# Edge pass of a graph attention kernel: the masked sum moves from the end of TensorE's step to its front

## The chip, the cores and the metric

The kernel runs on one core of a Trainium2 chip. Times are device microseconds (us) of one launch. A core has five engines that run their own instruction streams and meet at semaphores: TensorE (PE in the rows, with PEld for its weight loads), VectorE (DVE), ScalarE (ACT), GpSimd (POOL) and SyncE (SP, which here issues DMAs).

## The reference

The input is x with 50,000 rows of 768 numbers and a list of 25,000 edges (src, dst), sorted by dst. First comes a graph attention layer with 12 heads of 64, then a feed-forward layer:

```
def gnn(h, src, dst):                      # h = layernorm(x)
    ft = einsum('nhd,od->nho', h, W)
    e = leaky_relu(a1[src] + a2[dst])      # a1, a2: sums of ft times attention vectors
    w = exp(e - segment_max(e, dst)[dst])
    alpha = w / segment_sum(w, dst)[dst]
    agg = segment_sum(alpha * ft[src], dst)
    return relu(agg + einsum('nhd,od->nho', h, W_res))
x = x + gnn(layernorm(x), src, dst)
x = x + ffn(layernorm(x))                  # 768 -> 96 -> 768 for all but six rows
```

## The kernel before

The program has two long passes and a short passage between them. The **edge pass** computes `alpha * ft[src]` and its sum over edges of one destination, and writes one row of 768 per edge to a scratch tensor in memory, of which the **node pass** gathers what it needs. The node pass (392 tiles of 128 nodes) does the residual product and the feed-forward layer, and the change doesn't touch it.

The edge pass takes the edges in 196 chunks of 128 (`EC`). It is a pipeline written out by hand: every engine runs the same loop over steps c (14 steps in a loop body, `BODY`), and in step c it does the part with lag L for chunk c - L. What is done in which step is set by the `L_` constants, and in which order within a step by the order of the code. Nothing reorders it later. The engines' steps carry the same number c but aren't in lockstep; semaphores tie them.

TensorE's step c, lines 771 to 844: 12 transposes of the gathered source and destination rows of chunk c - 9 (L785), six products with the weights for chunk c - 10 (L794, called ft below), in some steps two small transposes (L811/L812 or L817/L818), six products that give the destination score of chunk c - 10 (L823, called a2 below), and last the masked sum of chunk c - 21 (L835 and L837, `L_SUM` = 21). The masked sum multiplies a 128x128 mask (edges with the same destination) by the weighted messages, and writes 768 columns to `sum_ps`, of which there is one (a second one, `sum2_ps`, is used only for the last ten chunks). So it waits for three things: the messages (`s_msg`), the mask (`s_mask`), and that the sum of the chunk before has been read out (`s_eo`).

VectorE's step c, in this order: small operations of a group of seven chunks (L1015 to L1046), the readout of the sum of chunk c - 22 into `agg_ring` (L1059, called evict below, 128x768; it waits for `s_sum` and for the DMA that wrote out the ring's slot two chunks ago), the messages of chunk c - 20 (L1071), four bn_stats and two bn_aggr of chunk c (L1106 to L1114), then a wait for a2 of the same step (`s_sc`), and behind it the mask of chunk c - 20 (L1128), the score column `e_col` of chunk c - 10 (L1149), and, each in one step of seven, the leaky maximum (L1157), the scans of the maximum (L1132 to L1172), the scans of the sum (L1177 to L1183) and the reciprocal with alpha (L1137 to L1144). The wait stands in the code as

```
                    if exists(cf, EC):
                        dve.wait_ge(s_sc, cf + 1)
```

with cf = c - 10, ahead of the mask. ScalarE reads the transposes (L665) and ft (L671) out of PSUM and normalizes (L651). GpSimd issues three indirect DMAs per chunk: a gather of source rows (L538), one of destination rows (L542) and a scatter of row numbers (L553), 13 to 15 chunks ahead and held back by `s_tr`, `s_sc` and `s_sum`. SyncE writes each evicted chunk to memory (L458).

Of the kernel before, what the change touches and what calls it, by code (L numbers as in the profile page):

```python
# [8 lines left out]
D = 768  # L9
# [5 lines left out]
P = 128  # L15
NC = D // P
# [11 lines left out]
BODY = 2 * G  # L28
EC = -(-N_EDGES // (P * BODY)) * BODY
# [19 lines left out]
L_FT = 10  # L49
L_DT = 20  # L50
L_MSG = 20
L_SUM = 21
# [21 lines left out]
def turns(eng, n, drain):  # L74


    yield 0
    yield 1
    if n > 2:
        with eng.Fori(2, n) as b:  # L80
            yield b
    for b in range(drain):
        yield n + b
# [7 lines left out]
def exists(t, n):  # L91

    return not isinstance(t, int) or 0 <= t < n


def at_least(eng, sem, value):

    if not isinstance(value, int) or value > 0:
        eng.wait_ge(sem, value)


def gnn_ffn_kernel(nc, x, x_cols, edges, dst_rows, dst_next, dst_prev, dst_ends, chunk_base, sel_heads,
# [9 lines left out]
    with ExitStack() as ctx:  # L112
# [3 lines left out]
        def sem(name):  # L116
            return ctx.enter_context(nc.semaphore(name))
# [10 lines left out]
        def part(lo, *shape, rows=P):  # L128
            size = 1
            for s in shape:  # L130
                size *= s
            flat = arena[0:rows, lo:lo + size]
            if len(shape) == 2:
                return flat.rearrange("p (a b) -> p a b", b=shape[1])
            if len(shape) == 3:
                return flat.rearrange("p (a b c) -> p a b c", b=shape[1], c=shape[2])
            return flat
# [4 lines left out]
        ft_ring = part(21504, BODY, NC, FTW)  # L142
        mask_ring = part(32424, 2, P)
# [120 lines left out]
        def sums(b, co):  # L264

            return sum2_ps if isinstance(b, int) and co > EC - L_SUM + L_FT and (EC - 1 - co) % 2 == 1 else sum_ps

        def twice(b, co):

            return 1 if isinstance(b, int) and co > EC - L_SUM + L_FT + 1 else 0  # L270
# [60 lines left out]
        s_eft = sem("s_eft")  # L331
        s_sc = sem("s_sc")
        s_ecol = sem("s_ecol")
        s_mask = sem("s_mask")
# [15 lines left out]
        s_msg = sem("s_msg")  # L350
        s_sum = sem("s_sum")
        s_eo = sem("s_eo")
# [399 lines left out]
        def _(pe):  # L752
# [5 lines left out]
            for c in range(NC):  # L758
                last = nc.tensor.matmul(ps[:, 1, 0:2 * HEADS], ones[:], v_sb[:, OFF * c:OFF * c + OFF],
                                        start=(c == 0), stop=(c == NC - 1))  # L760
# [10 lines left out]
            for b in turns(pe, NB, 2):  # L771
                for i in range(BODY):
                    c = BODY * b + i
                    ct = c - L_TR
                    if exists(ct, EC):
                        v = (i - L_TR) % BODY
                        for k in range(NBLK):
                            if k == 0:
                                pe.wait_ge(s_norm, ct + 1)
                            if k == 1:  # L780
                                pe.wait_ge(d_ge[v], 32 * (b + (i - L_TR) // BODY + 1))
                            at_least(pe, s_etr, NBLK * (ct - 1) + k + 1)
                            for m in range(4 * k, 4 * k + 4):
                                src = xs_ring if m < NC else xd_ring
                                last = nc.tensor.transpose(ps[:, k, m % 4 * P:(m % 4 + 1) * P],  # L785
                                                           src[:, v, m % NC * P:(m % NC + 1) * P], ident[:])
                            last.then_inc(s_tr, 1)
                    cf = c - L_FT
                    if exists(cf, EC):
                        v = (i - L_FT) % 2  # L790
                        pe.wait_ge(s_etr, NBLK * cf + 2)
                        at_least(pe, s_eft, cf)
                        for n in range(NC):
                            last = nc.tensor.matmul(ft_ps[:, n // 3, n % 3, :], both_t[:, v, n * P:(n + 1) * P],  # L794
                                                    wgv[:, n, :], start=True, stop=True)
                        last.then_inc(s_ft, 1)

                    gs_ = 2 * b + (i - 18) // G
                    ga = 2 * b + (i - 20) // G
                    if exists(cf, EC + 1):  # L800
                        at_least(pe, s_ecol, cf)
                    if (i - 18) % G == 0 and exists(gs_, NG):
                        pe.wait_ge(s_same, gs_ + 1)
                    if (i - 20) % G == 0 and exists(ga, NG):
                        pe.wait_ge(s_alpha, ga + 1)
                    gt_ = 2 * b + (i - 17) // G
                    if (i - 17) % G == 0 and exists(gt_, NG):
                        w = (i - 17) // G % 2
                        pe.wait_ge(s_leak, gt_ + 1)
                        pe.wait_ge(s_dsl, gt_ + 1)  # L810
                        nc.tensor.transpose(row_ps[:, 0:P], e_col[:, w, :], ident[:])  # L811
                        nc.tensor.transpose(row_ps[:, P:2 * P], same_x[:, w, :], ident[:]).then_inc(s_ert, 1)  # L812
                    gw_ = 2 * b + (i - 19) // G
                    if (i - 19) % G == 0 and exists(gw_, NG):
                        pe.wait_ge(s_exp, gw_ + 1)
                        pe.wait_ge(s_tot, gw_ + 1)
                        nc.tensor.transpose(w_ps, w_row[:], ident[0:HG, 0:HG])  # L817
                        nc.tensor.transpose(den_ps, m_row[:], ident[0:HG, 0:HG]).then_inc(s_wst, 1)  # L818
                    if exists(cf, EC):
                        v = (i - L_FT) % 2  # L820
                        pe.wait_ge(s_etr, NBLK * cf + NBLK)
                        for n in range(NC):
                            last = nc.tensor.matmul(a2_ps, both_t[:, v, D + n * P:D + (n + 1) * P],  # L823
                                                    v2c[:, n, :], start=(n == 0), stop=(n == NC - 1))
                        last.then_inc(s_sc, 1)
                    co_ = c - L_SUM
                    if exists(co_, EC):
                        v = (i - L_SUM) % BODY
                        pe.wait_ge(s_msg, co_ + 1)
                        pe.wait_ge(s_mask, co_ + 1)  # L830
                        at_least(pe, s_eo, co_ - twice(b, co_))
                        if isinstance(b, int) and co_ == EC - L_SUM + L_FT + 1:
                            pe.wait_ge(s_eft, EC)
                        to = sums(b, co_)
                        nc.tensor.matmul(to[:, 0:4 * P].rearrange("p (a f) -> p a f", f=P), mask_ring[:, v % 2, :],  # L835
                                         ft_ring[:, v, 0:4, 0:P], start=True, stop=True)
                        nc.tensor.matmul(to[:, 4 * P:D].rearrange("p (a f) -> p a f", f=P), mask_ring[:, v % 2, :],  # L837
                                         ft_ring[:, v, 4:NC, 0:P], start=True, stop=True).then_inc(s_sum, 1)
                    if isinstance(b, int) and c == EC + 14:
                        pe.wait_ge(s_eqf, 1)  # L840
                        for n in range(2):
                            last = nc.tensor.matmul(cnt_ps[:, n:n + 1], eq_f[:, n * EH:(n + 1) * EH], ones[:, 0:1],
                                                    start=True, stop=True)
                        last.then_inc(s_cnt, 1)
# [27 lines left out]
            for b in turns(pe, NT // U, 1):  # L872
                for u in range(U):
# [7 lines left out]
                    if exists(tu, NT):  # L881
                        q = b * (U // PAIR) + (u - L_UP) // PAIR
                        v, k = (u - L_UP) // PAIR % 2, (u - L_UP) % PAIR
# [3 lines left out]
                        for i in range(k * NC // PAIR, (k + 1) * NC // PAIR):  # L887
                            for n, (w, h) in enumerate(((w1_hi, t2_hi[:, v]), (w1_lo, t2_hi[:, v]), (w1_hi, t2_lo[:, v]))):
                                last = nc.tensor.matmul(ps[0:HID, 6 + v, 0:PAIR * P], w[:, i, :], h[:, i, :],  # L889
                                                        start=(i == 0 and n == 0), stop=(i == NC - 1 and n == 2))  # L890
# [3 lines left out]
                    if exists(td, NT):  # L894
                        v = (u - L_DOWN) // PAIR % 2
                        f = slice((u - L_DOWN) % PAIR * P, ((u - L_DOWN) % PAIR + 1) * P)
                        pe.wait_ge(s_hlo, b * (U // PAIR) + (u - L_DOWN) // PAIR + 1)
                        at_least(pe, s_o, td)
                        for lo, hi in ((0, 512), (512, D)):
                            for n, (h, w) in enumerate(((h_hi, w2_hi), (h_hi, w2_lo), (h_lo, w2_hi))):  # L900
                                last = nc.tensor.matmul(pair(2)[:, lo:hi], h[:, v, f], w[:, lo:hi],  # L901
                                                        start=(n == 0), stop=(n == 2))
# [14 lines left out]
            for a in range(NEXP):  # L917
                for i in range(NC):
                    last = nc.tensor.matmul(ps[0:HID, 0, a * NCLS:(a + 1) * NCLS], a1_sb[:, i, a, :], cls_t[:, i, :],  # L919
                                            start=(i == 0), stop=(i == NC - 1))  # L920
            last.then_inc(s_ch, 1)
            for i in range(NC):
                last = nc.tensor.matmul(ps[0:NCLS, 1, 0:2 * NCLS], cls_t[:, i, :], gw_sb[:, i, :],
                                        start=(i == 0), stop=(i == NC - 1))
# [3 lines left out]
            for s in range(2):  # L928
                for lo, hi in ((0, 512), (512, D)):
                    for a in range(NEXP):  # L930
                        last = nc.tensor.matmul(pair(1 + s)[0:NCLS, lo:hi], hm[:, s, a, :], a2_sb[:, a, lo:hi],  # L931
                                                start=(a == 0), stop=(a == NEXP - 1))
# [441 lines left out]
```

## Time and profile before

| | before |
|---|---|
| median of 3 runs | 2899.18 us |
| lowest and highest | 2893.96, 2901.88 us |
| the profiled execution's own time | 2880.44 us |
| its span | 2878.2 us |
| edge pass with all parts running, from the end of the last a2 ahead of the first sum to the end of the last a2 | 117.88 to 1133.73 us |
| busy over the span: TensorE, VectorE, ScalarE, GpSimd | 95%, 90%, 76%, 74% |
| mean granted clock of TensorE | 0.978 of full |

The profile is of one execution. Its table gives the busy time of each engine; the timeline gives every instruction with its start, its length and, in brackets, how long its engine had been idle and what ended that. A granted clock of 1.00 in a stretch stands for 2.4 GHz and 0.50 for 1.2 GHz; the values between are means over a stretch in which both occurred.

### The profile page before, as it was taken

The numbers are of one execution on the slowest core, as the hardware profiler recorded it, in microseconds if no ns is written. First come the engines' busy times: TensorE is split into PE (matmuls) and PEld (weight loads), VectorE is DVE, ScalarE is ACT, GpSimd is POOL, SyncE is SP. The second block draws the span as 40 slices with busy tenths as digits, with TensorE's granted clock in tenths as the row PEclk, the third lists the DMA queues.
The fourth block names the chain that finished last, engine by engine and source line by source line (L and its number), as shares of the span: only waits on it lengthen the run. The fifth ranks groups of instructions, "written<-read, shape, count | busy, mean of one in ns | idle before, by whom it ended". The sixth has DMA issues, their size and how long they took to land. (4 is left out here: it accounts for less than half of the span.)

```text
span 2878.2 us, 67583 instructions
## 1 busy us (share of the span) xinstructions
PE 2739.4 (95%) x21062; PEld 2543.4 (88%) x21062; DVE 2579.1 (90%) x5419; ACT 2179.7 (76%) x4157; POOL 2136.6 (74%) x2029
## 2 busy tenths in 40 slices
PE   4789999999999998489999999999999999999998
PEld 4777888888888887389999999999999999999996
DVE  5677899999999996589999999999999999999995
ACT  3545566666666664389999999999999999999982
POOL 6755666677767650388888888888888888888881
PEclk9899999999999999699999999999999999999998
DMA  8999999999888872689999999999999998989973
GB/s 209 173 194 193 219 234 230 235 231 236 233 232 238 231 199 102 232 300 345 341 334 328 328 322 323 319 319 319 318 309 317 314 315 310 312 311 312 309 268 120
DMA packets 254693, 770.85 MB, mean 268 GB/s; under 512 B 79795, under 2 KB 85683, under 8 KB 254355
## 3 DMA queue, kind: packets, MB, share of 16 engines
q1 hardware_dynamic: 181964, 557.25, 55.2%
q0 software_dynamic: 69312, 209.33, 31.9%
q8 instruction: 122, 2.00, 0.3%
q10 hardware_dynamic: 3176, 1.29, 0.2%
q14 instruction: 119, 0.97, 0.1%
HBM read 635.88 MB, written 232.17 MB: 302 GB/s over the span
## 5 line engine op out<-in xcount | busy, mean ns | idle before, releaser
L910 PE MATMUL ps<-wr_bd,arena 128*128 128x128 f32 x4704 | 594.4, 276 | 25.7 <-DVE arena L1254 23.0
L910 PEld LDWEIGHTS ps<-wr_bd,arena 128*128 128x128 f32 x4704 | 564.0, 193 | 28.4 <-issue 25.1
L632 POOL DMA_INDIRECT arena<-agg_scratch,nrow x392 | 440.1, 1123 | 82.2 <-issue 67.7
L665 ACT ACTIVATE arena<-ps 128x512 f32<-128x512 f32 x588 | 308.1, 594 | 189.4 <-PE ps L785 188.8
L610 POOL TENSOR_SCALAR arena<-csr_neg,mv,r_n 128x768 f32<-128x768 f32 x392 | 388.1, 990 | 50.8 <-PE ps L768 36.7
L1249 DVE SCALAR_TENSOR_TENSOR ps<-ps,r_n,arena 128x768 f32<-128x768 f32 x392 | 398.9, 1018 | 19.3 <-PE ps L910 11.2
L1254 DVE SCALAR_TENSOR_TENSOR arena<-ps,arena 128x768 f32<-128x768 f32 x392 | 375.3, 957 | 13.4
L622 POOL TENSOR_SCALAR arena<-arena,nm_n,r_n 128x768 f32<-128x768 f32 x392 | 384.1, 980 | 0.8 <-POOL r_n L601 0.6
L713 ACT ACTIVATE t_hi<-ps 128x768 fp32r<-128x768 f32 x392 | 315.2, 804 | 88.5 <-PE ps L768 88.2
L1261 DVE TENSOR_TENSOR t_lo<-ps,t_hi 128x768 fp32r<-128x768 f32 x392 | 373.7, 953 | 6.7 <-ACT t_hi L713 6.5
L701 ACT ACTIVATE arena<-arena,mv 128x768 f32<-128x768 f32 x392 | 368.0, 939 | 12.7
L1238 DVE TENSOR_TENSOR arena<-arena,ps 128x768 f32<-128x768 f32 x392 | 369.8, 943 | 6.2 <-PE ps L901 6.1
L722 ACT ACTIVATE arena<-arena,s_st 128x768 f32<-128x768 f32 x392 | 364.3, 929 | 11.5 <-DVE arena L1254 11.5
L889 PE MATMUL ps<-t_hi,w_hi 128*96 128x256 f32 x1176 | 360.9, 307 | 0.0
L889 PE MATMUL ps<-t_lo,w_hi 128*96 128x256 f32 x1176 | 330.3, 281 | 0.0
L785 PE MATMUL ps<-ident,arena 128*128 128x128 f32 x2352 | 298.1, 278 | 33.2 <-ACT arena L651 23.2
L889 PE MATMUL ps<-t_hi,w_lo 128*96 128x256 f32 x1176 | 328.7, 280 | 0.0
L768 PE MATMUL ps<-ident,arena 128*128 128x128 f32 x2352 | 322.1, 273 | 5.9 <-POOL arena L622 5.4
L739 ACT ACTIVATE arena<-arena 128x768 f32<-128x768 f32 x392 | 326.1, 832 | 0.6
L785 PEld LDWEIGHTS ps<-ident,arena 128*128 128x128 f32 x2352 | 277.9, 144 | 53.4 <-issue 24.7
L542 POOL DMA_INDIRECT arena<-in_x,e_slot x196 | 192.2, 981 | 173.3 <-PE ps L823 127.5
L794 PE MATMUL ps<-wgv,arena 128*128 128x130 f32 x2352 | 298.5, 276 | 0.0
(199 smaller groups left out, 6361.7 us busy)
## 6 DMA issues: line engine op xcount, KB each, us to landing
arena<-in_x SPq DMA_DIRECT2D x196, 768.0 KB
arena<-in_x_cols SPq DMA_DIRECT2D x392, 384.0 KB, 4.9
out<-arena SPq DMA_DIRECT2D x195, 768.0 KB, 5.7
agg_scratch<-arena SPq DMA_DIRECT2D x196, 384.0 KB, 2.3
dst_all<-in_dst_rows SPq DMA_DIRECT2D x28, 256.0 KB
arena<-in_x,e_slot POOLq DMA_INDIRECT x392, 6.7
arena<-agg_scratch,nrow POOLq DMA_INDIRECT x392
dst_all<-in_dst_rows SPq DMA_DIRECT2D x28, 192.0 KB
```

The costliest lines, as they stand in the source:

```text
L610: pool.tensor_scalar(g_ring[:, g, :].rearrange("p (c f) -> p c f", f=P), csr_neg[:, None, :].to_broadcast([P, NC, P]), mv1[:, w, 2 * (v % ...
L622: pool.tensor_scalar(n2[:, v % 2, :], y_ring[:, v, :], nm_n[:, w, k:k + 1], r_n[:, w, PAIR + k:PAIR + k + 1], ALU.add, ALU.mult).then_inc( ...
L632: pool.indirect_dma_start(g_ring[:, g, :], None, agg_d, bass.IndirectOffsetOnAxis(nrow[:, v:v + 1], 0), bounds_check=EP - 1, oob_is_err=Fa ...
L701: nc.scalar.activation(junk[:, 0, :], x_ring[:, v, :], ACT.Square, bias=mv1[:, w, 2 * k:2 * k + 1], scale=-1.0, accum_out=q_st[:, w, k:k + ...
L722: nc.scalar.activation(junk[:, 1, :], y_ring[:, v, :], ACT.Square, bias=s_st[:, w, k:k + 1], scale=-float(D), accum_out=q_st[:, w, 2 + k:3 ...
L785: last = nc.tensor.transpose(ps[:, k, m % 4 * P:(m % 4 + 1) * P], src[:, v, m % NC * P:(m % NC + 1) * P], ident[:])
L889: last = nc.tensor.matmul(ps[0:HID, 6 + v, 0:PAIR * P], w[:, i, :], h[:, i, :], start=(i == 0 and n == 0), stop=(i == NC - 1 and n == 2))
L910: last = nc.tensor.matmul(pair(1)[:, i * P:(i + 1) * P], xt_ring[:, g, i * P:(i + 1) * P], wr_bd[:], start=True, stop=True)
L1238: V.tensor_tensor(y_ring[:, v, :], y_ring[:, v, :], pair(2), ALU.add).then_inc(s_o, 1)
L1249: V.scalar_tensor_tensor(pair(1), pair(1), r_n[:, w, k:k + 1], g_ring[:, g, :], ALU.mult, ALU.add).then_inc(s_z1, 1)
L1254: V.scalar_tensor_tensor(y_ring[:, v, :], pair(1), 0.0, x_ring[:, v, :], ALU.max, ALU.add, accum_out=s_st[:, w5, k:k + 1]).then_inc(s_y, 1)
L1261: V.tensor_tensor(t2_lo[:, v, :, f], pair(0).rearrange("p (c n) -> p c n", c=NC), t2_hi[:, v, :, f].bitcast(f32), ALU.subtract).then_inc(s ...
```

## The change

The block that makes the masked sum is moved, word for word, from the end of TensorE's step to its front, ahead of the transposes. The lag stays 21.

```diff
             for b in turns(pe, NB, 2):
                 for i in range(BODY):
                     c = BODY * b + i
+                    co_ = c - L_SUM
+                    if exists(co_, EC):
+                        v = (i - L_SUM) % BODY
+                        pe.wait_ge(s_msg, co_ + 1)
+                        pe.wait_ge(s_mask, co_ + 1)
+                        at_least(pe, s_eo, co_ - twice(b, co_))
+                        if isinstance(b, int) and co_ == EC - L_SUM + L_FT + 1:
+                            pe.wait_ge(s_eft, EC)
+                        to = sums(b, co_)
+                        nc.tensor.matmul(to[:, 0:4 * P].rearrange("p (a f) -> p a f", f=P), mask_ring[:, v % 2, :],
+                                         ft_ring[:, v, 0:4, 0:P], start=True, stop=True)
+                        nc.tensor.matmul(to[:, 4 * P:D].rearrange("p (a f) -> p a f", f=P), mask_ring[:, v % 2, :],
+                                         ft_ring[:, v, 4:NC, 0:P], start=True, stop=True).then_inc(s_sum, 1)
                     ct = c - L_TR
                     if exists(ct, EC):
...
                         last.then_inc(s_sc, 1)
-                    co_ = c - L_SUM
-                    if exists(co_, EC):
-                        v = (i - L_SUM) % BODY
-                        pe.wait_ge(s_msg, co_ + 1)
...
```

The block adds and removes no instruction; the streams of the other four engines are the same row by row. In the new file the transposes stand at L798, ft at L807, the small ones at L824/L825 and L830/L831, a2 at L836 and the sum at L783/L785.

TensorE where the sums begin, before. The first two rows are a2 of step 19 and the transposes of step 20, then step 21 with the first sum (chunk 0) at its end, and step 22:

```order
37 L823 MATMUL ps<-v2c,arena 128x12 x6
38 L785 MATMUL ps<-ident,arena 128x128 x12
39 L794 MATMUL ps<-wgv,arena 128x130 x6
40 L823 MATMUL ps<-v2c,arena 128x12 x6
41 L785 MATMUL ps<-ident,arena 128x128 x12
42 L794 MATMUL ps<-wgv,arena 128x130 x6
43 L823 MATMUL ps<-v2c,arena 128x12 x6
44 L835 MATMUL ps<-arena 128x512
45 L837 MATMUL ps<-arena 128x256
46 L785 MATMUL ps<-ident,arena 128x128 x12
47 L794 MATMUL ps<-wgv,arena 128x130 x6
48 L823 MATMUL ps<-v2c,arena 128x12 x6
```

The same place of the changed kernel:

```order
37 L836 MATMUL ps<-v2c,arena 128x12 x6
38 L798 MATMUL ps<-ident,arena 128x128 x12
39 L807 MATMUL ps<-wgv,arena 128x130 x6
40 L836 MATMUL ps<-v2c,arena 128x12 x6
41 L783 MATMUL ps<-arena 128x512
42 L785 MATMUL ps<-arena 128x256
43 L798 MATMUL ps<-ident,arena 128x128 x12
44 L807 MATMUL ps<-wgv,arena 128x130 x6
45 L836 MATMUL ps<-v2c,arena 128x12 x6
46 L783 MATMUL ps<-arena 128x512
47 L785 MATMUL ps<-arena 128x256
48 L798 MATMUL ps<-ident,arena 128x128 x12
```

In both the sum stands between an a2 and the next transposes, but its chunk is another: chunk 0 followed a2 of step 21 and now follows a2 of step 20, one whole step (transposes, ft, a2) earlier. From there on every sum comes one step earlier in TensorE's stream.

VectorE in the loop, the same in both: the end of a step and the front of the next, as far as its evict. The branch between them is the loop's turn:

```order
201 L1128 TENSOR_SCALAR arena<-dst_all,dst_slot 128x128
202 L1149 SCALAR_TENSOR_TENSOR e_col<-ps,r_a,arena 128x12
203 L80 UNCONDITIONAL_BRANCH
204 L80 ISA
205 L1031 TENSOR_SCALAR ve_a<-mvs 128x14
206 L1053 ISA
207 L1054 REGISTER_ALU
208 L99 ISA
209 L1059 SCALAR_TENSOR_TENSOR arena<-csr,nmd_b,ps 128x768
```

Nothing moved here: the mask waits for a2 of its step, and the evict, which frees `sum_ps`, stands behind it.

## Rows read from the trace of the kernel before

**Rows 1.** The page: busy us of each engine, share of the span, instructions.

```profile
PE 2739.4 (95%) x21062; PEld 2543.4 (88%) x21062; DVE 2579.1 (90%) x5419; ACT 2179.7 (76%) x4157; POOL 2136.6 (74%) x2029
```

**Rows 2.** Waits, 118 to 1134 us: who waited for whom, us, times, longest.

```profile
DVE arena L1059 <- DMA agg_scratch<-arena: 41.2, 19, 5.7
...
POOL row_scratch L553 <- PE ps L837: 28.7, 12, 5.9
...
PE ps L835 <- DVE arena L1059: 21.3, 13, 3.8
...
DVE arena L1059 <- PE ps L837: 16.4, 35, 1.0
```

**Rows 3.** Timeline, TensorE, 509 to 511 us: start, length, line, operation.

```profile
509.16 1.11 PE L835 MATMUL ps<-arena 128*128 128x512 f32 x2
...
510.11 0.59 PE L837 MATMUL ps<-arena 128*128 128x256 f32 x2
...
510.54 1.47 PE L785 MATMUL ps<-ident,arena 128*128 128x128 f32 x12
```

**Rows 4.** Timeline at the end of the edge pass, 1128 to 1137 us.

```profile
1128.36 1.40 PE L823 MATMUL ps<-v2c,arena 128*128 128x12 f32 x12
1128.55 0.82 ACT L671 ACTIVATE arena<-ps 128x780 f32<-128x780 f32 x1 [0.56 <-PE ps L794]
...
1129.80 0.29 DVE L1128 TENSOR_SCALAR arena<-dst_all,dst_slot 128x128 f32<-128x128 int32 x1 [2.01 <-PE ps L823]
...
1135.16 1.01 DVE L1059 SCALAR_TENSOR_TENSOR arena<-csr,nmd_b,ps 128x768 f32<-128x768 f32 x1 [0.68 <-PE ps L837]
...
1136.32 1.10 PE L835 MATMUL ps<-arena 128*128 128x512 f32 x2 [0.98 <-DVE arena L1059]
```

**Rows 5.** Windows, VectorE: start:end length, busy (instructions), PEclk, DMA share, GB/s.

```profile
971.16:971.58 0.42, 0.42 (x3) 1.00 1.19 168
1013.33:1014.28 0.95, 0.93 (x6) 1.00 0.59 230
381.59:382.01 0.42, 0.42 (x5) 1.00 0.96 395
349.73:350.36 0.63, 0.60 (x5) 1.00 1.05 400
274.62:276.84 2.22, 2.12 (x10) 1.00 1.00 396
735.74:737.23 1.49, 1.31 (x7) 1.00 1.36 307
517.53:519.09 1.56, 1.49 (x7) 1.00 1.07 154
513.47:517.53 4.06, 3.96 (x9) 1.00 0.81 240
```

**Rows 6.** Windows, TensorE, same columns: the edge pass, then eight single steps.

```profile
117.88:1133.73 1015.85, 992.13 (x7414) 0.99 0.87 215
117.88:124.78 6.90, 5.43 (x41) 1.00 0.84 161
199.96:206.74 6.78, 5.42 (x40) 1.00 0.75 136
135.96:145.35 9.39, 7.28 (x43) 0.82 0.93 198
145.35:156.26 10.91, 7.10 (x42) 0.84 0.90 250
161.55:169.41 7.86, 7.13 (x41) 0.78 0.87 101
174.70:183.92 9.22, 7.20 (x44) 0.81 0.85 222
212.18:223.39 11.21, 8.18 (x41) 0.70 0.99 209
258.17:268.99 10.82, 7.01 (x41) 0.84 0.81 190
```

More of the change, by code:

```diff
@@ L825, in _ @@
                         last.then_inc(s_sc, 1)
-                    co_ = c - L_SUM
-                    if exists(co_, EC):
-                        v = (i - L_SUM) % BODY
-                        pe.wait_ge(s_msg, co_ + 1)
[L830 to L838, printed above, removed]
                     if isinstance(b, int) and c == EC + 14:
```

## The prediction

> **What bounds the kernel now.** I began with the table of busy time: TensorE is busy for 95% of the span and VectorE for 90% [rows 1], so the reader should expect two engines near their limit, and ask who waits for whom. The window over the edge pass says it more sharply: from 117.88 to 1133.73 us TensorE is busy for 992.13 of 1015.85 us [rows 6]. These are 185 steps (21 to 205), so a step takes 1015.85 / 185 = 5.49 us. The timeline shows how closely they are packed: the sum starts at 509.16, its second half at 510.11, the next transposes at 510.54 [rows 3], one behind the other. The list of waits shows what little TensorE waits for: 21.3 us in 13 waits of the sum for the evict [rows 2]. Of these rows the reader is to see that today the sum rarely waits, because its predecessor's evict has nearly a whole step of TensorE's work as cover.
>
> **What is removed, added and moved.** No instruction comes or goes. In a ring of four parts (sum, transposes, ft, a2) the sum stays between a2 and transposes, and it now serves the chunk one step earlier. What counts is its three waits. In step c the sum is of chunk c - 21. The messages and the mask of that chunk come from VectorE's step c - 1, ahead of everything that follows. The third wait, s_eo, wants the evict of chunk c - 22, and that is in VectorE's step **c**, behind the end of its step c - 1, which waits for a2 of TensorE's step c - 1 (s_sc). So TensorE's a2 of step c - 1 is what the mask waits for, the evict stands behind the mask, and the sum ahead of TensorE's next transposes waits for the evict. The loop closes within a single step: sum, transposes, ft, a2, mask and e_col, evict, sum. Behind the waiting sum are queued TensorE's transposes, ft and a2; behind these wait ScalarE's readouts, VectorE's next mask and GpSimd's gathers. Before, a full step of TensorE's work lay between that evict and the sum that wants it.
>
> **TensorE's part of the loop**: from the start of a sum to the end of a2. Two steps that started after a gap and ran at full clock give it: 5.43 and 5.42 us busy, the second and third window of [rows 6]. I take 5.42.
>
> **VectorE's part**, during which TensorE now stands still. First, from the end of a2 to the mask: a2 ends at 1128.36 + 1.40 = 1129.76 and the mask, which had been idle for it, starts at 1129.80 [rows 4]: 0.04 us. ScalarE's readout of ft, which e_col also wants, is done at 1128.55 + 0.82 = 1129.37, earlier [rows 4]. Second, from the start of the mask to the start of the next evict. This has seven kinds, one for each place in the group of seven chunks, since the small group operations lie in this stretch. I looked for a place of each kind at which VectorE waited for nothing; the first seven windows of [rows 5] run from the start of a mask to the start of the evict behind it: 0.42, 0.95, 0.42, 0.63, 2.22 (maximum scans), 1.49 (sum scans), 1.56 (reciprocal and alpha), together 7.69, mean 1.10 us. Third, the evict itself, 1.01 us, and then 1136.32 - (1135.16 + 1.01) = 0.15 us until the sum starts [rows 4]. The mean gap is 0.04 + 1.10 + 1.01 + 0.15 = 2.30 us; for the seven kinds it is 1.62, 2.15, 1.62, 1.83, 3.42, 2.69 and 2.76.
>
> The rest of VectorE's step is covered: from the start of an evict to the next mask it needs 4.06 us with messages and statistics, the last window of [rows 5], whereas TensorE gets there only after 1.01 + 0.15 + 5.42 = 6.58 us. VectorE waits there for 2.5 us.
>
> **The loop alone**: 5.42 + 2.30 = 7.72 us a step, times 185 steps = 1428 us, less the 1015.85 that the stretch takes today: **+412 us**. The small transposes of two steps in seven are left out. The evict's waits for its ring slot (41.2 us in 19 waits, 5.7 at most, [rows 2]) I count at nothing: the write has two steps to land, and these grow by 2 x 2.2 us. If that fails, the same 41 us come on top; if these waits go, nothing is gained beyond what the loop already counts. GpSimd's scatter, which waited 28.7 us for the sum [rows 2], finds it a step earlier, which buys nothing on this loop. The waits of the evict for the sum, 16.4 us [rows 2], end too. The last ten chunks alternate between two sum buffers, and no a2 runs then, so the loop opens after step 205. Nothing else changes: the stretches ahead of 117.88 and behind 1133.73 keep their time.
>
> **TensorE's clock.** The gaps have a second price. At six places of the edge pass a gap stands behind an a2, and the granted clock of the step from that gap on is 0.70 to 0.84, so part of it ran at 1.2 instead of 2.4 GHz, the fourth to the ninth window of [rows 6]. Length less busy gives the gap: 2.11, 3.81, 0.73, 2.02, 3.03 and 3.81 us. At two places, with gaps of 1.47 and 1.36 us, the clock stayed at 1.00, the second and third window of [rows 6]. So all five gaps of 2 us or more lost the clock, and of the three shorter ones one did. In such a step the busy time is 7.28, 7.10, 7.13, 7.20, 8.18 and 7.01 instead of 5.42: 1.86, 1.68, 1.71, 1.78, 2.76 and 1.59 us more, median 1.75. Of the seven kinds of gap in the changed kernel four are over 2 us. The other three (1.62, 1.62, 1.83) lie between the rows on either side; I take the clock as lost in half of them. That is 5.5 steps of 7 at 1.75 us, 1.375 us a step, times 185 = **+254 us**. The bounds are nothing, and every step at the dearest, 2.76 x 185 = 511 us.
>
> The Trainium skill ("TensorE: Matmul & The Clock Gate", section "Why this matters for your kernels") has a rule of thumb for how long TensorE may idle between bursts without its clock falling, and of the seven gaps here only the 3.42 us one exceeds it. By that rule the clock term would be one step in seven, 185 / 7 x 1.75 = 46 us, and the time 3357 us. The rows speak against it, since the gaps of 2.02 and 2.11 us lost the clock.
>
> **Sum.** 2880.44 + 412 + 254 = 3546 us for an execution like the profiled one. The median of the runs shown is 2899.18, 18.74 us above that execution, so 3565 us is the forecast.
>
> **The rivals.**
>
> *The loop closes, and the clock holds.* For it: two gaps of 1.4 us left the clock alone, and the new gaps are regular, with 5.4 us of dense work between them, whereas those in the rows came in a stretch disturbed by late DMAs. Against it: the five gaps of over 2 us. Time: 2899 + 412 = 3311 us; with the clock lost only at the 3.42 us gap it is 3357. Chance 0.18.
>
> *The loop closes, and the clock is lost nearly everywhere, at times for longer.* A step at half clock makes its own a2 later, and the gap behind it comes at a clock that has barely risen; the 8.18 us step [rows 6] is of this kind. For it: even a gap of 0.73 us lost the clock once. Time between 3311 + 1.75 x 185 = 3635 us and 3311 + 511 = 3822 us. Chance 0.14.
>
> *The sum finds its predecessor read out* (not slower). TensorE's order is the same ring as before, so if VectorE made the evict before it waits for a2, the move would be free, and the 21.3 us of waits of the sum would be all that is at stake: between 2878 and 2899 us. It decides at one point, whether the evict of chunk c - 22 stands ahead of or behind the wait for a2 of step c - 1 in VectorE's stream. It stands behind, and the mask at 1129.80, idle for 2.01 us until a2 [rows 4], shows that this wait is real. The same goes for the rival that nothing is changed by the move because the ring is the same. Chance 0.06, of which 0.04 within 0.3% and 0.02 faster.
>
> **How the numbers follow.** The forecast, loop and clock lost in most steps, has 0.62, and its own range runs from four steps in seven at 1.59 us (168 us: 3479) to every step at 1.75 us and the 41 us of ring waits (3676). The range given takes in the rival with the held clock below and stops short of most of the dearest case: 3300 to 3700 us. It leaves out about 0.10 above and 0.06 below. Slower by over 0.3% (about what a measurement of this kernel can tell from no change) in all cases but the last rival: 0.94; within 0.3% 0.04; faster 0.02.
>
> **What would show each step.** In the new timeline the evict L1059 should be followed after 0.15 us by the sum (now L783), and the wait list should hold the sum waiting for L1059 some 185 times, near 420 us in all, with 3.4 us where the maximum scans lie and 1.6 us where nothing does. VectorE's mask should be idle for some 2.5 us for a2 (now L836) in each step. The window over the edge pass should be some 1680 us long, with a granted clock of 0.75 to 0.9; a clock of 0.98 or more there decides for the first rival. The node pass should keep its time. If the sum waits for less than 1 us in the mean, the loop is not closed, and the whole of the argument falls.

## The result, and the profile after

The changed kernel takes 3582.1 us (3579.9 to 3584.73) against 2896.57 us of the kernel before on the same chip: ratio 1.2369, 95% interval 1.2339 to 1.2399. The forecast was 3565 us, in a range of 3300 to 3700. The profiled execution took 3581.6 us, its span is 3579.4 us.

The page has the busy time of each engine, to be read against [rows 1]:

```profile
PE 3025.8 (85%) x21062; PEld 2761.7 (77%) x21062; DVE 2584.3 (72%) x5419; ACT 2212.9 (62%) x4157; POOL 2124.2 (59%) x2029
```

VectorE, ScalarE and GpSimd are as long busy as before, within 2%. TensorE has the same 21,062 instructions and is busy for 286 us more; its mean granted clock is 0.899 in place of 0.978. The waits over the whole span, where those rows were of the edge pass (who waited for whom, us in total, times, longest), which answer to [rows 2]:

```profile
DVE arena L1128 <- PE ps L836: 764.2, 185, 7.7
...
PE ps L783 <- DVE arena L1059: 435.1, 186, 3.5
...
DVE arena L1059 <- PE ps L785: 4.5, 6, 1.2
```

Of the kernel before, 118 to 1134 us, the mask's row reads

```profile
DVE arena L1128 <- PE ps L823: 18.8, 11, 2.2
```

The sum (L783) now waits for the evict (L1059) 186 times, in place of 13, and VectorE's mask (L1128) waits 185 times for a2 (L836), in place of 11. Each engine waits once a step for the other: this is the closed loop. The evict's waits for its ring slot, 41.2 us before, are gone from the list.

Timeline of one step at full clock (start, length, engine, line, in brackets the idle time ahead of it and what ended it):

```profile
722.50 1.10 PE L783 MATMUL ps<-arena 128*128 128x512 f32 x2 [1.61 <-DVE arena L1059]
...
723.86 1.47 PE L798 MATMUL ps<-ident,arena 128*128 128x128 f32 x12
...
725.17 1.51 PE L807 MATMUL ps<-wgv,arena 128*128 128x130 f32 x12
...
726.52 1.40 PE L836 MATMUL ps<-v2c,arena 128*128 128x12 f32 x12
727.96 0.29 DVE L1128 TENSOR_SCALAR arena<-dst_all,dst_slot 128x128 f32<-128x128 int32 x1 [2.51 <-PE ps L836]
728.16 0.23 DVE L1149 SCALAR_TENSOR_TENSOR e_col<-ps,r_a,arena 128x12 f32<-128x12 f32 x1
728.42 0.25 DVE L1157 SCALAR_TENSOR_TENSOR e_col<-e_col 128x84 f32<-128x84 f32 x1
728.58 1.01 DVE L1059 SCALAR_TENSOR_TENSOR arena<-csr,nmd_b,ps 128x768 f32<-128x768 f32 x1
...
729.74 1.10 PE L783 MATMUL ps<-arena 128*128 128x512 f32 x2 [1.82 <-DVE arena L1059]
```

Read it as a ring: TensorE works from 722.50 to 727.92 (5.42 us), 0.04 us later the mask starts, evict and all ahead of it take until 729.59, and 0.15 us later comes the next sum. Windows over the edge pass and two of its steps (length, TensorE busy with instructions, granted clock, DMA share, GB/s), to be read against [rows 6]:

```profile
122.51:1830.34 1707.83, 1276.80 (x7493) 0.83 0.48 129
722.50:729.74 7.24, 5.42 (x41) 1.00 0.66 126
823.03:832.25 9.22, 7.09 (x41) 0.81 0.39 130
```

These are the 185 steps from 21 to 205. The stretch that was measured before, 117.88 to 1133.73 us, holds only 183 of them, and not 185: the first sum starts at 112.45, and 117.88 is the end of a2 of step 22, behind it. The same 185 steps of the kernel before, from the end of a2 of step 20, are

```profile
108.65:1133.73 1025.08, 1001.36 (x7490) 0.99 0.87 215
```

So they take 1707.83 instead of 1025.08 us, 683 of the 701 us by which the span grew. Of the rest, 13.9 us lie ahead of step 21, where the moved block hasn't run yet, and 4.5 us behind the last a2. The kernel with lag 22 below has the 14 us too (its a2 of step 20 ends at 124.01 us) and isn't slower, so they aren't the loop's doing. The third window is a step of the other kind, from one sum to the end of the gap behind it: the same 41 instructions are busy for 7.09 instead of 5.42 us, at a mean clock of 0.81.

### The profile page after: what moved, and what is told of

Read it like the earlier page. It is cut to its first block and busy times, and to the rows that moved or that the text cites. A ratio compares the mean times of both kernels' runs of the same rounds, so it can differ in the third digit from the quotient of the medians.

```text
span 3579.4 us, 67584 instructions
## 1 busy us (share of the span) xinstructions
PE 3025.8 (85%) x21062; PEld 2761.7 (77%) x21062; DVE 2584.3 (72%) x5419; ACT 2212.9 (62%) x4157; POOL 2124.2 (59%) x2029
## 5 line engine op out<-in xcount | busy, mean ns | idle before, releaser
L665 ACT ACTIVATE arena<-ps 128x512 f32<-128x512 f32 x588 | 332.7, 597 | 846.8 <-PE ps L798 818.7
L783 PE MATMUL ps<-arena 128*128 128x512 f32 x392 | 279.6, 802 | 446.8 <-DVE arena L1059 435.1
L1128 DVE TENSOR_SCALAR arena<-dst_all,dst_slot 128x128 f32<-128x128 int32 x196 | 56.0, 286 | 764.2 <-PE ps L836 764.2
L538 POOL DMA_INDIRECT arena<-in_x,e_slot x196 | 193.7, 988 | 617.2 <-PE ps L798 588.1
L798 PEld LDWEIGHTS ps<-ident,arena 128*128 128x128 f32 x2352 | 416.6, 196 | 79.3 <-issue 63.3
L798 PE MATMUL ps<-ident,arena 128*128 128x128 f32 x2352 | 441.5, 361 | 34.0 <-ACT arena L651 23.9
L783 PEld LDWEIGHTS ps<-arena 128*128 128x128 f32 x392 | 70.2, 223 | 461.4 <-issue 433.0
L542 POOL DMA_INDIRECT arena<-in_x,e_slot x196 | 188.6, 962 | 314.7 <-PE ps L836 284.2
L722 ACT ACTIVATE arena<-arena,s_st 128x768 f32<-128x768 f32 x392 | 364.5, 930 | 13.9 <-DVE arena L1254 13.9
```

The costliest lines, as they stand in the source:

```text
L722: nc.scalar.activation(junk[:, 1, :], y_ring[:, v, :], ACT.Square, bias=s_st[:, w, k:k + 1], scale=-float(D), accum_out=q_st[:, w, 2 + k:3 ...
```

## Experiments

All ratios are against the kernel before, run on the same chip. Three chips were used, and its medians there were 2886.67, 2883.02 and 2862.84 us, so the ratios are compared, not the times. The changed kernel stands at 1.2369.

### One step later: is it the place in the code?

```diff
-L_SUM = 21
+L_SUM = 22
```

The sum stays at the front of TensorE's step, but for the chunk before.

> Sum at the front of the step as in the changed kernel, but L_SUM is 22 instead of 21, so each sum comes one step later and its predecessor's evict has a whole step of TensorE's work as cover again. Theory (the loop closes because the sum comes a step too early): the time of the kernel before, 2897 us within 0.5%, granted clock 0.97 or more. Rival (a wait at the head of TensorE's step is what costs, whichever chunk it is for): 3582 us, as the changed kernel.

Measured: 2880.26 us, ratio 0.9988 (0.9970 to 1.0007). Its waits in the edge pass, 118 to 1134 us, and the window over it:

```profile
PE ps L783 <- DVE arena L1059: 7.7, 10, 1.9
...
118.00:1134.00 1016.00, 1003.06 (x7522) 0.99 0.86 216
```

The sum waits 10 times for the evict, not 186, and the clock is back at 0.99. A wait at the head of the step costs nothing. What costs is which chunk is waited for.

### Which of the three waits closes the loop?

The block of the evict is moved in VectorE's step from the front to behind the statistics, ahead of the wait for a2, and works on chunk c - 21. The lines behind the `+` are the old block with another lag.

```diff
-                    ca = c - L_AGG
...
+                    ca = c - L_EVICT
...
                     if exists(cf, EC):
                         dve.wait_ge(s_sc, cf + 1)
```

(`L_EVICT` = 21.) Messages and mask stay where they are.

> The changed kernel, but VectorE makes the evict of the sum (chunk c - 21 instead of c - 22) in step c behind its statistics and ahead of its wait for a2 of that step. The sum itself stays at the front of TensorE's step with lag 21. Theory (of the sum's three waits it is the one for the evict that closes the loop, since the evict stands behind the wait for a2): the loop opens, the gaps and the clock's loss go, 2890 us within 1%, granted clock 0.97 or more. Rival (messages or mask, also made one step before, come too late for a sum at the front): the sum goes on waiting, now for L1071 or L1128; these come at the latest 0.2 us behind a2, so that even alone they would cost some 0.4 us a step, 2970 us, and more with the clock.

Measured: 3027.6 us, ratio 1.0503 (1.0481 to 1.0525). Timeline of a step:

```profile
704.40 0.97 DVE L1113 SCALAR_TENSOR_TENSOR arena<-csr,nmd_b,ps 128x768 f32<-128x768 f32 x1
705.29 1.40 PE L837 MATMUL ps<-v2c,arena 128*128 128x12 f32 x12
706.73 0.29 DVE L1129 TENSOR_SCALAR arena<-dst_all,dst_slot 128x128 f32<-128x128 int32 x1 [1.36 <-PE ps L837]
...
707.12 1.10 PE L784 MATMUL ps<-arena 128*128 128x512 f32 x2 [0.43 <-issue]
```

The evict (now L1113) is over at 705.37, 1.3 us ahead of the end of a2 (L837), and no longer holds the sum (L784). With it 0.187 of the 0.237 by which the changed kernel was slower is gone: the evict is the wait that closed the loop. But my main expectation, 2890 us, fell. The mask (L1129) stands behind the wait for a2, ends at 707.02, and the sum starts 0.10 us later, 0.43 us behind the end of a2. ("issue" says that the profile names no releaser; that it is the mask follows from the times here, and the next run confirms it.) That is the second dependency within one step, hidden so far behind the longer one. I had named it as the rival and put it at 0.4 us a step, 2970 us. It costs more, 0.0503 x 2883 / 185 = 0.78 us a step. The trace has TensorE idle for 0.56 us a step between a2 and the sum, 104 of the 145 us, up to 3.9 us at once, and the clock lost in 15 steps instead of 6. The rest stays open.

With the mask ahead of that wait too (the next experiment's edit on top):

> Both: evict ahead of the wait for a2, and the mask too. A try at a version faster than both kernels. If the loop is open with the early evict, the mask off the wait shortens what lies between a2 and the next a2 that needs e_col; since TensorE is busy for 97% of the edge pass, at most 1015.85 - 992.13 = 24 us are to be had against the kernel before: 2873 to 2897 us. Rival (VectorE, idle least in the open loop, is the bound): no difference to the early evict alone.

Measured: 2969.98 us, ratio 1.0292 (1.0264 to 1.0320). Neither expectation came: two fifths of what was left go, and the version isn't faster than the kernel before. TensorE's idle time between a2 and the sum falls from 0.56 to 0.27 us a step, 54 of the 61 us gained, so the mask was what the sum waited for in the run above. Its waits, 118 to 1230 us:

```profile
PE ps L784 <- DVE arena L1127: 54.3, 66, 4.3
```

The sum still waits 66 times for the mask (L1127), up to 4.3 us. VectorE's row is in the order messages, statistics, evict, mask. Right behind the step with the maximum scans lie 28.2 us of these waits, and 14.1 us behind that with the reciprocal: VectorE comes late there with its whole row, and the slack of a full step that the kernel before has isn't there. What else the 2.9% hold stays open; VectorE itself waits 41.2 us for ScalarE's readout of ft ahead of `e_col`.

### The mask alone off the loop

```diff
-                    if exists(cf, EC):
-                        dve.wait_ge(s_sc, cf + 1)
                     cd = c - L_DT
...
                         V.tensor_scalar(mask_ring[:, v % 2, :], dst_all[:, j * P:(j + 1) * P], dst_slot[:, w, j:j + 1], None,
                                         ALU.is_equal).then_inc(s_mask, 1)
+                    if exists(cf, EC):
+                        dve.wait_ge(s_sc, cf + 1)
```

> The changed kernel, with VectorE's wait for a2 moved from ahead of the mask to behind it, so the mask (0.20 us from its start to the next) leaves the loop. Theory: 185 x 0.20 = 37 us less by the loop, and with gaps of 1.4 to 1.6 us in three places of seven the clock is lost less often there (at most 38 steps x 1.89 = 72 us less): 3475 to 3545 us. Rival (the length of the gap doesn't count one to one, because the rest of the step takes up the slack): 3582 us.

Measured: 3499.9 us, ratio 1.2136 (1.2111 to 1.2161), that is 0.0233 x 2883 = 67 us less than the changed kernel, of the 37 to 109 expected. Over the 185 steps the gap between a2 and the sum is 0.19 us a step shorter (35 us in all), and TensorE is busy for 34 us less, with the clock lost in 130 steps instead of 138. The mean clock of the execution rose from 0.899 to 0.911, and the sum's waits for the evict fell from 435.1 to 387.2 us:

```profile
PE ps L783 <- DVE arena L1059: 387.2, 180, 3.3
```

The same edit on the kernel before, where no loop is closed:

> The kernel before (sum at the end of the step), with VectorE's mask ahead of its wait for a2, as in the run on the changed kernel where it took 82 us off. Theory (the mask pays only where it stands on a closed loop; here TensorE is busy for 97% of the edge pass): within 0.3% of the kernel before; at best the 16 us that VectorE's evict waits for the sum, 0.6% faster. Rival (VectorE's order is worth its time in the kernel before too): 185 x 0.2 = 37 us or more, 1.3% faster.

Measured: 2862.77 us, ratio 1.0001 (0.9989 to 1.0014). The same 0.2 us of VectorE is worth 2% in one kernel and nothing in the other. (The 82 us in the expectation are the plain difference of two medians from different chips; by the ratios it is 67 us.)

### The same operation on the loop and off it

One more VectorE operation, on constants, in 174 steps ahead of the evict's wait, and in 176 steps behind the messages. Its result goes into a buffer that only the node pass uses.

```diff
+                        if exists(c, EC):
+                            V.scalar_tensor_tensor(t2_hi[:, 0, 0:3, :].rearrange("p a (b f) -> p (a b) f", f=P),
+                                                   csr[:, None, :].to_broadcast([P, NC, P]), half[:, 0:1],
+                                                   csr[:, None, :].to_broadcast([P, NC, P]), ALU.mult, ALU.add)
                         dve.wait_ge(s_sum, ca + 1)
```

> The changed kernel, with one more VectorE operation of 128x768 (SBUF to SBUF, about 0.95 us) ahead of each evict for 174 steps, so between a2 and the sum. Theory (that stretch of VectorE is on the loop): 174 x 0.95 = 165 us more, and the clock lost in nearly all steps, up to 0.25 x 1.75 x 174 = 76 us more: 3750 to 3825 us. Rival (VectorE is idle for 764 us in its wait for a2 and hides it): 3582 us.

> The changed kernel, with the same extra VectorE operation, but behind the messages, where the theory says VectorE's work is covered (it idles some 2.5 us a step in its wait for a2, and more at half clock). Theory: no change, 3582 us within 0.5%. Rival (what counts is VectorE's total work, or the operation disturbs others wherever it stands): 165 us more, 3747 us.

Measured: on the loop 3802.14 us, ratio 1.3169 (1.3137 to 1.3202); off it 3588.84 us, ratio 1.2441 (1.2412 to 1.2470). The costliest groups of instructions show the added work of the two (line, operation, tiles, count, busy us, mean ns, idle before):

```profile
L1054 DVE SCALAR_TENSOR_TENSOR t_hi<-csr,half 128x768 fp32r<-128x768 f32 x174 | 175.7, 1010 | 0.0
```

```profile
L1075 DVE SCALAR_TENSOR_TENSOR t_hi<-csr,half 128x768 fp32r<-128x768 f32 x176 | 178.3, 1013 | 0.0
```

And the waits, first with the operation on the loop (mask L1132, evict L1063), then off it:

```profile
DVE arena L1132 <- PE ps L836: 822.3, 186, 8.0
...
PE ps L783 <- DVE arena L1063: 589.4, 186, 4.3
```

```profile
DVE arena L1132 <- PE ps L836: 611.9, 185, 7.6
...
PE ps L783 <- DVE arena L1059: 435.2, 186, 3.5
```

On the loop, TensorE waits 154 us longer for the evict (589.4 against 435.1), which is 0.89 us for each added operation. Of the remaining 77 of the 231 us (0.0800 x 2887), 58 us are longer busy time of TensorE, whose clock is now lost in 169 of the 185 steps instead of 138; the last 19 us I leave open. Off the loop, TensorE's wait is 435.2 us, the same to a tenth, and VectorE's own wait for a2 is shorter by 152 us, so it absorbed nearly all of the work. The ratio is 0.6% above that of the changed kernel (1.2441 / 1.2369), and the two intervals don't overlap: no change within 0.5% was expected, and that was narrowly missed. Of these 21 us, 11 are longer busy time, since 143 steps lost the clock instead of 138. Why, and where the other 10 lie, stays open.

### What the clock costs

TensorE gets constant work for the gap: 7 to 14 products of 120 columns ahead of the sum's waits, into bank 0 of PSUM, which is free there.

```diff
                         v = (i - L_SUM) % BODY
+                        if exists(c - L_TR, EC):
+                            pe.wait_ge(s_etr, NBLK * (c - L_TR - 1) + 1)
+                            for _ in range((7, 9, 7, 7, 14, 11, 11)[i % G]):
+                                nc.tensor.matmul(ps[:, 0, 0:120], ident[:], wgv[:, 0, 0:120], start=True, stop=True)
                         pe.wait_ge(s_msg, co_ + 1)
```

> The changed kernel, with 7 to 14 extra products of 120 columns (by the place in the group of seven) into a free PSUM bank ahead of each sum's waits, so that TensorE works through most of the gap (1.5 to 3.1 us of the 1.6 to 3.5) and is there when the evict ends. Theory (the gap costs its length and, on top, the clock): the loop stays, the clock is held, and the clock's share goes: busy time of a step from 6.83 back to 5.42 us, 185 x 1.41 = 261 us less, 3321 us. Rival 1 (the longer busy time has another cause, as PSUM or SBUF traffic): no gain, 3582 us. Rival 2 (the extra products themselves come late or run at half clock and delay the sum): above 3582 us.

Measured: 3363.46 us, ratio 1.1662 (1.1639 to 1.1685). Timeline of TensorE over a step with the longest gap, and the window over the edge pass:

```profile
715.99 1.41 PE L840 MATMUL ps<-v2c,arena 128*128 128x12 f32 x12
717.25 3.36 PE L780 MATMUL ps<-wgv,ident 128*128 128x120 f32 x28
720.80 1.10 PE L787 MATMUL ps<-arena 128*128 128x512 f32 x2 [0.19 <-DVE arena L1063]
...
120.90:1612.00 1491.10, 1435.41 (x10952) 0.98 0.58 148
```

The added products (L780) end 0.19 us before the evict lets the sum go. The granted clock of the edge pass is 0.98 in place of 0.83, and from the start of a sum to the end of a2 a step is now busy for 5.52 us in the mean (6.90 in the changed kernel; the 6.83 of the expectation was read from pieces of the timeline and is a little low), 1.38 x 185 = 255 us less. The kernel became faster by adding 1732 products whose results nobody reads, and the loss of the clock is thereby measured by itself. The time fell by 0.0707 x 2887 = 204 us only, because the work came late at some places:

```profile
PE ps L780 <- issue: 28.7, 11, 4.4
```

Eleven times TensorE idled up to 4.4 us ahead of it for nothing that the trace shows. The eleven places lie 112.8 to 115.6 us apart, which is 14 steps of this kernel: it happens once per turn of the loop. The gap between a2 and the next sum, which holds these waits and the steps in which the added work outlasts the gap, is 2.53 us in the mean, against 2.33 in the changed kernel: 0.20 x 185 = 37 us of the 51 that are missing. Why TensorE is late at the turn stays open.

### The evict early in the kernel before

The same move of the evict, with the sum at the end of TensorE's step.

> The kernel before (sum at the end of TensorE's step), with the evict of chunk c - 21 in VectorE's step c ahead of its wait for a2. Now the evict waits for a sum that stands behind a2 in TensorE's step, and the mask and e_col stand behind the evict; the next a2 wants that e_col, but transposes and ft (2.7 us) lie between as cover for evict, mask and e_col (1.0 + 0.04 + 0.5 us), except where the scans lie. Theory: open loop, 2887 us, at most 1.5% slower from VectorE's waits for the sum. Rival (any evict in that place helps, whatever the sum's place): as fast as the changed kernel with the early evict or faster.

Measured: 2937.39 us, ratio 1.0182 (1.0154 to 1.0211). The waits, 118 to 1180 us, show the new dependency: VectorE's evict (L1113) waits for the sum (L838), and the mask and e_col with it.

```profile
DVE arena L1113 <- PE ps L838: 90.7, 95, 3.1
```

So the early place makes this kernel slower, and helps only where the sum is early too. I had put the cost at 1.5% at most; it is a little more. The rival's number, as fast as 1.0503 or faster, would hold as well and doesn't decide; what speaks against the rival is that the ratio is above 1.

## Why the prediction was right, point by point

**The loop.** The step that carried the forecast was that the evict the sum waits for stands in VectorE's stream behind the wait for a2 of the step just ended. The 186 waits of the sum and the 185 of the mask show it, and the experiments with lag 22 and with the early evict show that it is this dependency that costs most: 0.187 of the 0.237. The mask's is next, with 0.021.

**The length of the gap.** Forecast 2.30 us in the mean; measured (1707.83 - 1276.80) / 185 = 2.33. By kinds, in the forecast's order, the last five have medians of 1.61, 1.82, 3.41, 2.69 and 2.75 us against 1.62, 1.83, 3.42, 2.69 and 2.76, all within 0.03 us. The first two were put too low: 1.77 or 2.13 us against 1.62, and 2.09 or 2.32 against 2.15, by the half of the 14-step body that the step lies in. At three of these four places the mask starts 0.20 instead of 0.04 us behind a2; I had taken that latency from a single step, the one at 1129.76. And at one place of the first kind L1031 and the turn of VectorE's loop lie between mask and evict, 0.86 instead of 0.42 us. Fourteen kinds should have been read, and not seven.

**TensorE's clock.** This was the term with the widest bounds, 0 to 511 us, and the largest risk. Forecast: the clock lost behind all gaps over 2 us and half of those under it, 145 of 185 steps, at 1.75 us each. I counted the steps of the new trace that are busy for over 6.0 us: they stand behind 102 of the 113 gaps of 2.1 to 3.5 us, and behind 35 of the 71 gaps of 1.5 to 1.9 us; with the first step they are 138. They are busy for 7.39 us in the mean and the others for 5.47, so each costs 1.92 us; 1.75 was the median of six in the forecast, whose mean was 1.90. Together 138 x 1.92 = 265 us against the 254 of the sum. The number came this close partly by luck: too many steps at too low a price, and the half for the short gaps was a guess between the rows on either side of them. The 8.18 us step was also misread. The forecast's dearest rival gave it as one whose gap came at a clock that had barely risen, but the step ahead of it, 206.74 to 212.18 us, ran at 1.00.

**The base of the loop term.** The 412 us compare 185 steps with a stretch that holds 183. With the 1025.08 us of the same 185 steps the loop alone is 1428 - 1025 = 403 us, 9 less. The time of a step before is 1015.85 / 183 = 5.55 us, and not 5.49.

**The rest.** The evict's waits for its ring slot were counted at nothing, and there are none left. The scatter's waits for the sum are gone too. The sum was 666 us for the profiled execution; it took 701 us more. The 35 us between them are, rounded, 6 us of longer gaps, 11 us of clock, 10 us of small transposes, which the forecast left out, and 18 us outside the 185 steps, where it had forecast no change, less the 9 us by which the base was too short. Of the signs, the window is 1708 us (1680 forecast), its clock 0.83 and the sum's waits 435 us (420). The mask's idle time is 2.5 us only in steps at full clock, as in the one shown; in the mean it is 764.2 / 185 = 4.1 us, since TensorE takes longer in the others.

The rule of the Trainium skill ("TensorE: Matmul & The Clock Gate", section "Why this matters for your kernels") on idle gaps would have given 3357 us. This case's trace disagrees with it: the clock fell behind 76 of 87 gaps of 2.1 to 2.8 us and behind 35 of 71 shorter ones. The rival with the held clock, 3311 us or 1.142 times the kernel before, is what the kernel with the added products comes near to (1.166), so its price was about right and its condition wasn't met.

## What to carry to other kernels

Moving a step of a hand-written pipeline within its loop changes its lag by one against every engine that it waits for, even if the order on its own engine looks the same: for each wait find the signalling instruction in the other engine's stream, and ask what that engine waits for ahead of it. When two engines wait for each other once per step, the step is the sum of both parts, and an operation of 1.01 us on that ring cost 0.89 us a step here, with the clock on top, while the same work beside it cost almost nothing. To open such a ring, move the release of the buffer or the consumer by one step; and look for the next dependency of the same kind before promising the whole gain.

## What the runs showed of the hardware that I had not expected

TensorE's clock fell behind short pauses: in the changed kernel it ran at 1.2 GHz for part of the step behind 35 of 71 gaps of 1.5 to 1.9 us, and behind 102 of 113 gaps of 2.1 to 3.5 us. Behind the short ones it mattered what the step before had done: 31 of the 53 gaps whose step before had lost the clock lost it again, and 4 of the 18 others. Products without use in the pauses kept it at 0.98 and made the kernel 6% faster.
